# A fused token, state-space and expert kernel: rows of C spread by DMA, scan states in PSUM, and both residual sums moved into TensorE's accumulations

## The chip, the core and the metric

The kernel runs on one core of a Trainium2 chip. The metric is the device time of one execution in microseconds (us), the median of repeated runs; lower is better. Engine names in the profile: PE is TensorE's matmuls and PEld its weight loads, DVE is VectorE, ACT is ScalarE, POOL is GpSimd, SP is the engine that issues the DMAs. `Lnnn` is a line of the kernel.

## What is computed

The whole model is a tokenizer (convolutions over 32 images), a state-space (Mamba) layer with a gated feed-forward part, and a layer of attention with routed experts. The change is in the middle layer. Cut to what matters, for tokens in 32 sequences of 82:

```python
xdbl = z @ W_xproj.T                       # -> dt_in (96), B (16), C (16) per token
dt   = softplus(dt_in @ W_dt.T + b_dt)     # (.., 384)
A_bar = exp(dt[..., None] * A)             # (.., 384, 16)
Bx    = (dt * z)[..., None] * B[:, None, :]
h[t]  = A_bar[t] * h[t-1] + Bx[t]          # the scan, along a sequence
y     = sum_s h[..., s] * C[..., s] + D_skip * z
x1    = xl + y @ W_out.T                   # first residual
x     = (x1 + H) + ffn(rmsnorm(x1))        # second residual, written back to H
```

## The kernel before

Four sequences make a round (328 tokens), so the middle layer has 8 rounds. In a round the 16 states of `y` are taken one after another: 16 *turns*, `s` = 0 to 15. The 384 channels lie as 3 groups of 128 partitions, so one turn handles tiles of 128x984. In turn `s` of round `i`:

- ScalarE writes the decays `exp(dt*A)` of turn `s+2` into two PSUM banks (`decays`, L1198), in two halves. The first half may start once the first half of the scan of turn `s+1` has read the bank, and this scan waits for nothing else there.
- GpSimd multiplies `dtz` with a row of B that a DMA has copied to all partitions (`Bb`), giving `Bx`, three turns ahead (L1450).
- VectorE multiplies the states `hs` with the row of C (*the product*, L1343), then runs the scan of turn `s+1` in two halves of 492 (L1333). `hs` has four buffers in SBUF (`LONG`), so a scan needs no wait for the product just ahead of it. The row of C stands in PSUM, where TensorE has spread it over the partitions with a selecting matmul (`spread_c`, L1030) from a split into three bf16 pieces, `P3`. The pieces are made by ScalarE (L1145, L1149, L1150), VectorE (`R`, L1289) and GpSimd (L1416).
- TensorE adds the product to `y` in PSUM by a matmul with the identity (`add_y`, L1050), and in turn 15 also `D_skip * z` (L1048).

Around this stand the side works of the neighbouring rounds, in an order written out by hand (`program`): in turn `s` of round `i` come `post(s)` of round `i-1` and `pre(s)` of round `i+1`. TensorE and ScalarE do them ahead of their own `step`, VectorE and GpSimd behind it. Every engine works strictly in the order of its list, and semaphores hold it. What the prediction speaks of:

- turn 0: ScalarE copies `y` out of PSUM (`drain`, L1216) when `add_y` of turn 15 is done. TensorE's next `add_y` waits for this copy.
- turn 1: TensorE multiplies `y` with `w_o` into O0 and O1 (L997). VectorE adds `xl` and writes `x1` (L1309). ScalarE makes `hn` for the next round (L1131).
- turn 2: TensorE transposes `hn` (L949), into the banks that O0 and O1 had; it waits until `x1` is taken out. ScalarE scales the result to `hT` (L1103, L1106), and its decays of turn 4 stand behind that.
- turns 3 to 5: `z` (L1285); turn 6: TensorE computes B, C and dt_in (L979) and ScalarE copies them out (L1144 to L1146); turns 8 to 11: softplus, the longer part of it on GpSimd.
- turns 10 to 13: the feed-forward part in four slices, TensorE, then ScalarE's tanh, then VectorE's `th` and `av` (L1314, L1317).
- turn 14: TensorE multiplies `av` with `w_dn` into N0 and N1 (L1022), behind the last `av`. VectorE adds `x1` and writes `H` (L1323) in turns 14 and 15.

The last round has no `pre`, and its `post(14)`, `post(15)` and the whole `post` of the last round follow in a function `ending`, mixed with the first parts of the attention layer. Ahead of the first scan stand VectorE's statistics of 24 images (`chunk_stats`, L1269) and a first `pre` (L1292 to L1302).

## Time and profile before

| | |
|---|---|
| median of 3 runs | 1364.94 us (1364.93 to 1366.9) |
| the profiled execution, own time | 1364.19 us |
| its span, first to last instruction | 1362.2 us |
| the 8 rounds of the middle layer | from 253.01 us (first scan) to 763 us (last product) |
| start of product 0 in rounds 0 to 7 | 255.30, 315.36, 381.38, 446.58, 510.81, 575.87, 640.23, 704.95 us |

The profiled execution is 0.75 us below the median. Rounds 1 to 6 are 64.2 to 66.0 us long each. Within a round no engine is busy all the time; which wait ends last at a place is read from the chain of waits and the timeline.

### The profile page before, as it was taken

How to read it: one execution, taken by the hardware profiler on the slowest of the kernel's cores; microseconds unless marked ns; L12 is line 12 of the kernel's file. 1: busy time of each engine (PE TensorE's matmuls, PEld its weight loads, DVE VectorE, ACT ScalarE, POOL GpSimd, SP SyncE). 2: the span in 40 equal slices, each digit the busy share in tenths (PEclk: the TensorE clock that was granted, in tenths of full speed). 3: DMA queues.
4: the chain of work that ended last, by engine and by line, in shares of the span. 5: the costliest groups of instructions: out<-in, count | busy, mean ns of one | idle time of the engine just before them, and what ended most of it. 6: DMA issues, size and time to landing. Idle time of an engine off the chain costs nothing.

```text
span 1362.2 us, 20654 instructions
## 1 busy us (share of the span) xinstructions
PE 1196.6 (88%) x5844; PEld 759.2 (56%) x5845; DVE 1066.6 (78%) x2275; ACT 710.4 (52%) x1652; POOL 744.2 (55%) x473
## 2 busy tenths in 40 slices
PE   7986867478898989899997789999999889999996
PEld 4432434224454545455452468888888666667674
DVE  5998697998999999999989645677788756666663
ACT  1256431776868777787866334555553462323232
POOL 3047651877878796969697420115545665232322
PEclk9897878698999999999999998999998899999998
DMA  6200002440404041322320025001112133222221
GB/s 186 60 1 0 28 9 63 157 149 1 149 1 149 12 137 39 110 75 74 108 73 1 1 93 186 9 9 25 27 26 56 37 61 54 41 37 39 39 39 21
DMA packets 72573, 81.11 MB, mean 60 GB/s; under 512 B 13450, under 2 KB 65129, under 8 KB 72489
## 3 DMA queue, kind: packets, MB, share of 16 engines
q1 hardware_dynamic: 53154, 69.17, 16.0%
q0 software_dynamic: 17152, 9.24, 5.0%
q10 hardware_dynamic: 2184, 1.72, 0.5%
q8 instruction: 36, 0.59, 0.2%
q14 instruction: 47, 0.39, 0.1%
HBM read 48.75 MB, written 30.01 MB: 58 GB/s over the span
## 4 chain that ended last, share of the span: by engine, by line
PE 56%; DVE 20%; ACT 12%; issue 7%; POOL 2%; DMA 2%; DVEq 1%; SPq 0%; ACTq 0%; POOLq 0%
PE ps L1050 7%; PE ps L2295 6%; DVE hs L1333 5%; PE ps L2273 5%; PE ps L1652 3%; PE ps L1710 3%; PE ps L1022 3%; ACT ps L1198 3%; PE ps L2278 3%; PE ps L277 3%; PE ps L955 2%; PE ps L1725 2%; PE ps L2285 2%; PE ps L270 2%; PE ps L997 2%
## 5 line engine op out<-in xcount | busy, mean ns | idle before, releaser
L1450 POOL TENSOR_TENSOR Bx<-dtz,Bb 128x984 f32<-128x984 f32 x128 | 287.7, 2272 | 47.6 <-DVE hs L1333 34.4
L1333 DVE TENSOR_TENSOR_SCAN hs<-ps,Bx 128x492 f32<-128x492 f32 x256 | 287.7, 1165 | 15.9 <-POOL Bx L1450 12.2
L1050 PE MATMUL ps<-hs,b_id 128*128 128x492 f32 x512 | 236.9, 586 | 8.5 <-ACT y L1216 7.2
L1198 ACT ACTIVATE ps<-dt,A 128x324 f32<-128x324 f32 (+1 forms) x512 | 210.5, 456 | 56.3 <-DVE hs L1333 53.6
L2431 POOL DMA_INDIRECT out<-yt,dest x48 | 74.7, 1556 | 158.9 <-DVE yt L2417 149.2
L2350 ACT ACTIVATE hT__6147<-ps,e_b 128x128 f32<-128x128 f32 x288 | 79.4, 374 | 154.1 <-PE ps L2285 154.0
L1343 DVE TENSOR_TENSOR hs<-hs,ps 128x984 f32<-128x984 f32 x128 | 150.4, 1175 | 2.8 <-issue 0.6
L1050 PEld LDWEIGHTS ps<-hs,b_id 128*128 128x128 f32 x512 | 93.4, 195 | 75.3 <-issue 69.6
L2295 PE MATMUL ps<-W,hT__6147 128*128 x576 | 109.4, 327 | 1.0 <-DVE yb L2411 1.0
L2126 POOL DMA_INDIRECT buckets<-XS,c_slot x64 | 90.6, 1416 | 31.9 <-issue 16.4
L2138 POOL TENSOR_TENSOR c_x<-c_x,bro 82x192 f32<-82x192 f32 x32 | 18.9, 590 | 135.7 <-DVE c_x L1893 135.1
L2295 PEld LDWEIGHTS ps<-W,hT__6147 128*128 128x128 f32 x576 | 91.5, 191 | 1.7 <-issue 1.7
L1030 PE MATMUL ps<-P,sel 128*128 128x328 bf16 x128 | 40.2, 316 | 52.8 <-DVE hs L1343 40.8
L2397 DVE COPY hb<-ps 128x768 f32<-128x768 f32 x41 | 39.3, 958 | 59.2 <-PE ps L2278 58.1
L2273 PE MATMUL ps<-W,xT 128*128 x192 | 78.5, 534 | 6.1 <-DVE xT L2388 2.8
L1866 DVE TENSOR_REDUCE mx<-ps 82x12 f32<-82x984 f32 x32 | 37.7, 1178 | 56.0 <-PE ps L1710 55.3
L1030 PEld LDWEIGHTS ps<-P,sel 128*128 128x128 bf16 x128 | 12.3, 97 | 102.0 <-DVE hs L1343 67.4
L1725 PEld LDWEIGHTS ps<-V,PT 82*82 82x82 f32 x768 | 61.3, 154 | 7.6 <-issue 2.0
L1710 PE MATMUL ps<-kB,qT 128*82 128x328 f32 (+1 forms) x256 | 60.8, 382 | 3.1 <-DVE E L1870 2.0
L1725 PE MATMUL ps<-V,PT 82*82 82x17 f32 x768 | 60.3, 224 | 1.2 <-DVE XN L1900 1.2
...
L207 DVE SCALAR_TENSOR_TENSOR ps<-PF,vec,ps 96x196 f32<-96x196 f32 (+2 forms) x168 | 57.7, 423 | 0.0
...
## 6 DMA issues: line engine op xcount, KB each, us to landing
Bb<-b_rows SPq DMA_DIRECT2D x32, 656.0 KB, 6.8
...
```

Source lines behind the costliest of these rows:

```text
L1050: mm = pe.matmul(ps[:, BANK_Y + h, 0:HALF], ident[:], f2(hs[:, s % LONG])[:, h * HALF:(h + 1) * HALF], start=s == 0, stop=s == STATE - 1)
L1198: a = act.activation(ps[:, BANK_A + h, c:c + w].rearrange("p (g t) -> p g t", t=S)[:, :, 1:S], dt[:, (par + t // STATE) % 2, m, g0 * S:g1 ...
L1333: v.tensor_tensor_scan(f2(hs[:, t % LONG])[:, c], ps[:, BANK_A + h, 0:HALF], f2(Bx[:, t % RING])[:, c], 0.0, ALU.mult, ALU.add).then_inc(s ...
L1343: v.tensor_tensor(hs[:, s % LONG], hs[:, s % LONG], ps[:, BANK_C + s % 2, 0:N].rearrange("p (a n) -> p a n", a=1).broadcast_to([128, NI, N ...
L1450: g.tensor_tensor(Bx[:, t % RING], dtz[:, p], Bb[:, p, t % STATE, :].rearrange("p (a n) -> p a n", a=1).broadcast_to([128, NI, N]), ALU.mu ...
L1710: mm = pe.matmul(ps[0:S, SCORES + h0 // 6, (h0 % 6) * S:(h0 % 6 + h1 - h0) * S], qT[:, par, m_, q * S:(q + 1) * S], kB[:, par, m_, q, j:j ...
L1725: mm = pe.matmul(ps[0:S, HEAD_OUT + c % 2, h * (DH + 1):(h + 1) * (DH + 1)], PT[:, c % 2, h, :], V[:, vpar, c, h, :], start=True, stop=True)
L2126: g.indirect_dma_start(out=xs, out_offset=bass.IndirectOffsetOnAxis(ap=slot[:, p % 2, k, c:c + 1], axis=0), in_=slots(p)[:, c, :], in_offs ...
L2273: pe.matmul(ps[:, UP + h, 0:384], xT[:, p, 0, :], W1[:, bass.ds(e, 1), h * 384:(h + 1) * 384].rearrange("p a n -> p (a n)"), start=True, s ...
L2295: mm = pe.matmul(ps[:, Y, 0:D], hT[:, p, k, :], W2[:, k, bass.ds(e, 1), :].rearrange("p a n -> p (a n)"), start=k == 0, stop=k == KF - 1)
L2350: a = act.activation(hT[:, p, k, :], ps[:, FLIPPED + k // 3, (k % 3) * 128:(k % 3 + 1) * 128], ACT.Gelu, bias=b1[:, k, bass.ds(e, 1)])
L2431: g.indirect_dma_start(out=out, out_offset=bass.IndirectOffsetOnAxis(ap=dest[:, p:p + 1], axis=0), in_=yt[:, p, :], in_offset=None, comput ...
```

## The change

Three things. (1) B and C both go to DRAM (`bc_d`) and come back by DMA to all partitions, in one tile `BC` of four groups, which is now single and not one for each parity of the round; `spread_c`, `P3`, `Pm`, `R`, `sel` and `oh` are gone. (2) The scan writes its states to PSUM banks 2 and 3 (one buffer), and the product writes to `hc` in SBUF (four buffers). The scan of a turn therefore waits for the product ahead of it. (3) The residuals `xl` and `x1` are added by TensorE, as a matmul with the identity at the head of the accumulation (L994 and L1023 of the new file), and ScalarE copies the sums out (L1156 for `x1`, in turn 2; L1181 for `H`, in turn 15); VectorE's four sums of a round are gone. In `ending`, GpSimd's fills of `kB`, `XS` and `inc` wait for the last product.

```diff
         def _(sp):
...
-                sp.wait_ge(s_Bs, j + 1)
+                sp.wait_ge(s_BCs, j + 1)
                 if j >= 2:
                     sp.wait_ge(s_bx, (j - 1) * STATE)
-                sp.dma_start(b_d[par], Bs[:]).then_inc(s_bd, 16)
+                sp.dma_start(bc_d[par], BCs[:]).then_inc(s_bd, 16)
                 sp.wait_ge(s_bd, 16 * (j + 1))
+                rows = bc_d[par].rearrange("(a k g s) n -> a g k s n", a=1, k=2, s=GROUP)
                 for g in range(STATE // GROUP):
-                    rows = slice(g * GROUP, (g + 1) * GROUP)
-                    sp.dma_start(Bb[:, par, rows, :],
-                                 b_d[par, rows, :].rearrange("(a s) n -> a s n", a=1).broadcast_to([128, GROUP, N])).then_inc(s_Bb[g], 16)
+                    if j >= 1:
+                        sp.wait_ge(s_hc, (j - 1) * STATE + (g + 1) * GROUP)
+                    sp.dma_start(BC[:, g], rows[:, g].broadcast_to([128, 2, GROUP, N])).then_inc(s_BC[g], 16)
...
 TensorE, post
                 if s == 1:
-                    pe.wait_ge(s_y, p + 1)
+                    pe.wait_ge(s_xl, (p + 1) * G)
                     for h in range(2):
                         free(f"O{h}", p, other)
+                        pe.matmul(ps[0:S, bank(f"O{h}"), 0:2 * D], ident[0:S, 0:S], xl[:, par, 2 * h:2 * h + 2, :], start=True, stop=False)
+                        if h == 0:
+                            pe.wait_ge(s_y, p + 1)
...
                 if s == 14:
+                    pe.wait_ge(s_add, p + 1)
                     pe.wait_ge(s_av, p * 4 + 4)
                     for h in range(2):
                         if not is_last(p):
                             free(f"N{h}", p, other)
+                        pe.matmul(ps[0:S, wide(f"N{h}", p), 0:2 * D], ident[0:S, 0:S], x1[:, 2 * h:2 * h + 2, :], start=True, stop=False)
...
 TensorE, step
-                if not last or s + 2 < STATE:
-                    spread_c(i, par, s + 2)
                 add_y(i, par, s)
...
 ScalarE, pre(6) and pre(7)
-                    act.activation(Bs[:], ps[96:96 + STATE, bank("X"), 0:N], ACT.Copy).then_inc(s_Bs, 1)
-                    act.activation(P3[96:128, par, :], ps[96:128, bank("X"), 0:N], ACT.Copy).then_inc(s_hi, 1)
+                    act.activation(BCs[:], ps[96:96 + 2 * STATE, bank("X"), 0:N], ACT.Copy).then_inc(s_BCs, 1)
                     act.activation(dtin[:], ps[0:HD, bank("X"), 0:N], ACT.Copy).then_inc(s_dtin, 1)
-                if s == 7:
-                    act.wait_ge(s_R, j + 1)
-                    act.activation(P3[32:64, par, :], R[:], ACT.Copy)
-                    act.activation(Pm[:], R[:], ACT.Copy).then_inc(s_mid, 1)
...
 ScalarE, post
+                if s == 2:
+                    for h in range(2):
+                        act.wait_ge(s_o, p * 2 + (h + 1))
+                        act.activation(x1[:, 2 * h:2 * h + 2, :].rearrange("p j c -> p (j c)"), ps[0:S, bank(f"O{h}"), 0:2 * D], ACT.Copy).then_inc(s_x1, 1)
...
+                if s == 15:
+                    for h in range(2):
+                        act.wait_ge(s_dn, p * 2 + (h + 1))
+                        act.activation(H[:, bass.ds(p * G + 2 * h, 2), :].rearrange("p j c -> p (j c)"), ps[0:S, wide(f"N{h}", p), 0:2 * D], ACT.Copy).then_inc(s_H, 1)
...
 ScalarE, ending
             def ending(last):
+                post(last - 1, 0, 15, None)
                 drain(last)
+                post(last, 1, 2, None)
                 post(last, 1, 3, None)
...
 VectorE, post(1), post(14), post(15), pre(6) and the cast of sel in tail: removed; scan and step
                     if h == 0:
                         v.wait_ge(s_bx, i * STATE + (t + 1))
-                        at_least(v, s_ys, i * STATE + (t - LONG + 1))
+                        at_least(v, s_hc, i * STATE + t)
                     c = slice(h * HALF, (h + 1) * HALF)
-                    v.tensor_tensor_scan(f2(hs[:, t % LONG])[:, c], ps[:, BANK_A + h, 0:HALF], f2(Bx[:, t % RING])[:, c],
+                    v.tensor_tensor_scan(hs[:, c], ps[:, BANK_A + h, 0:HALF], f2(Bx[:, t % RING])[:, c],
                                          0.0, ALU.mult, ALU.add).then_inc(s_scan, 1)
...
                 v.wait_ge(s_scan, 2 * (i * STATE + s) + 2)
-                v.wait_ge(s_pc, i * STATE + (s + 1))
-                v.tensor_tensor(hs[:, s % LONG], hs[:, s % LONG],
-                                ps[:, BANK_C + s % 2, 0:N].rearrange("p (a n) -> p a n", a=1).broadcast_to([128, NI, N]),
+                at_least(v, s_ys, i * STATE + (s - LONG + 1))
+                v.tensor_tensor(hc[:, s % LONG], hs.rearrange("p (a n) -> p a n", a=NI),
+                                BC[:, s // GROUP, 1, s % GROUP, :].rearrange("p (a n) -> p a n", a=1).broadcast_to([128, NI, N]),
                                 ALU.mult).then_inc(s_hc, 1)
...
 GpSimd, ending
-                fr.fills(g)
+                fr.fills(g, lambda: g.wait_ge(s_hc, ROUNDS * STATE))
```

How the lists of the engines change is shown at three places. First TensorE at turns 14 and 15. Before, from the `w_dn` matmuls to the last `add_y` of the round:

```order
L1022 MATMUL ps<-wdn,av 82x192 x16
L640 REGISTER_ALU
L1030 MATMUL ps<-P_120,sel 128x328
L1050 MATMUL ps<-hs,b_id 128x492 x2
L640 REGISTER_ALU
L1030 MATMUL ps<-P_120,sel 128x328
L1048 MATMUL ps<-z,skip 128x328
L1048 MATMUL ps<-z,skip 128x164 x2
L1048 MATMUL ps<-z,skip 128x328
L1050 MATMUL ps<-hs,b_id 128x492 x2
```

After (`x_130` is `x1`, `b_id` the identity):

```order
L1023 MATMUL ps<-x_130,b_id 82x384
L1027 MATMUL ps<-wdn,av 82x192 x8
L1023 MATMUL ps<-x_130,b_id 82x384
L1027 MATMUL ps<-wdn,av 82x192 x8
L1037 REGISTER_ALU
L1046 MATMUL ps<-hc,b_id 128x492 x2
L1037 REGISTER_ALU
L1044 MATMUL ps<-z,skip 128x328
L1044 MATMUL ps<-z,skip 128x164 x2
L1044 MATMUL ps<-z,skip 128x328
L1046 MATMUL ps<-hc,b_id 128x492 x2
```

Two identity matmuls of 384 columns have come in, and two selecting matmuls of 328 bf16 columns are gone. The second place is TensorE at turns 0 and 1 of the next round. Before:

```order
L640 ISA
L1030 MATMUL ps<-P_120,sel 128x328
L1050 MATMUL ps<-hs,b_id 128x492 x2
L942 REGISTER_ALU
L997 MATMUL ps<-wo,y 82x192 x6
L942 REGISTER_ALU
L997 MATMUL ps<-wo,y 82x192 x6
L640 REGISTER_ALU
L1030 MATMUL ps<-P_120,sel 128x328
L1050 MATMUL ps<-hs,b_id 128x492 x2
```

After:

```order
L1037 ISA
L1046 MATMUL ps<-hc,b_id 128x492 x2
L991 REGISTER_ALU
L942 REGISTER_ALU
L994 MATMUL ps<-xl,b_id 82x384
L1000 MATMUL ps<-wo,y 82x192 x6
L942 REGISTER_ALU
L994 MATMUL ps<-xl,b_id 82x384
L1000 MATMUL ps<-wo,y 82x192 x6
L1037 REGISTER_ALU
L1046 MATMUL ps<-hc,b_id 128x492 x2
```

Again two identity matmuls more, here in the middle of the `w_o` matmuls, and two selecting ones fewer. The third place is ScalarE behind the last decays of the last round. Before:

```order
L1216 ACTIVATE y<-ps 128x984
L1172 ACTIVATE hf,b_ss<-x_135 82x192 x4
L1175 ACTIVATE b_ms<-b_ss 82x4
L1179 ACTIVATE hf<-x_135,b_rr 82x192 x4
L732 ACTIVATE qb<-vec 128x3
```

After:

```order
L1181 ACTIVATE H<-ps 82x384 x2
L1209 ACTIVATE y<-ps 128x984
L1156 ACTIVATE x_130<-ps 82x384 x2
L1161 ACTIVATE hf,b_ss<-x_130 82x192 x4
L1164 ACTIVATE b_ms<-b_ss 82x4
```

The copies of `H`, which wait for the `w_dn` matmuls, now stand ahead of the copy of `y`, for which the `w_o` matmuls wait.

## Rows read from the trace of the kernel before

**Rows 1.** Windows: stretch, its us, busy us (instructions) PE, PEld, DVE, ACT, POOL; PE clock, DMA share, GB/s.

```profile
303.00:319.00 16.00, 11.78 (x24) 5.30 (x22) 12.40 (x12) 6.91 (x16) 15.92 (x8) 0.57 0.00 1
...
446.60:510.80 64.20, 59.00 (x228) 31.99 (x227) 60.09 (x64) 47.81 (x114) 51.59 (x25) 1.00 0.25 79
```

**Rows 2.** Chain of waits, round 1 into round 2: start us, us, what.

```profile
372.42 0.51 DVE av L1317
...
373.06 5.40 PE ps L1022 x32
378.46 0.14 PE ps L1030
...
383.73 1.00 ACT y L1216
...
384.87 1.89 PE ps L1050 x4
386.76 3.90 PE ps L997 x24
...
390.80 1.65 PE ps L1050 x4
```

**Rows 3.** Timeline behind it: start us, us, engine line op tiles [idle before].

```profile
390.69 0.55 DVE L1309 TENSOR_TENSOR x<-xl,ps 82x384 f32<-82x384 f32 x1 [1.40 <-PE ps L997]
...
394.43 1.63 ACT L1198 ACTIVATE ps<-dt,A 128x324 f32<-128x324 f32 x4
...
395.63 2.25 DVE L1333 TENSOR_TENSOR_SCAN hs<-ps,Bx 128x492 f32<-128x492 f32 x2
```

**Rows 4.** Timeline of VectorE, turns 9 and 10 of round 1.

```profile
349.49 2.25 DVE L1333 TENSOR_TENSOR_SCAN hs<-ps,Bx 128x492 f32<-128x492 f32 x2 [0.29 <-ACT ps L1198]
351.78 1.18 DVE L1343 TENSOR_TENSOR hs<-hs,ps 128x984 f32<-128x984 f32 x1
352.88 2.25 DVE L1333 TENSOR_TENSOR_SCAN hs<-ps,Bx 128x492 f32<-128x492 f32 x2
```

**Rows 5.** Groups by form: count, busy us, mean ns, idle ahead and releasers.

```profile
L1333 DVE TENSOR_TENSOR_SCAN hs<-ps,Bx 128x492 f32<-128x492 f32 x256 | 287.7, 1165 | 15.9 <-POOL Bx L1450 12.2 <-ACT ps L1198 3.6
...
L207 DVE SCALAR_TENSOR_TENSOR ps<-P,vec,ps 128x196 f32<-128x196 f32 x168 | 56.4, 421 | 0.0
...
L207 DVE SCALAR_TENSOR_TENSOR D<-P,vec,ps 128x196 f32<-128x196 f32 x24 | 8.9, 413 | 0.0
L1309 DVE TENSOR_TENSOR x<-xl,ps 82x384 f32<-82x384 f32 x16 | 8.7, 549 | 13.8 <-PE ps L997 13.8
```

**Rows 6.** Timeline of VectorE ahead of the first scan.

```profile
229.14 1.40 DVE L508 SCALAR_TENSOR_TENSOR P<-P,rs,rows 105x192 f32<-105x192 f32 x4
233.70 0.50 DVE L1289 TENSOR_TENSOR R<-ps,P 32x328 f32<-32x328 f32 x1 [3.16 <-ACT P L1145]
...
234.34 2.17 DVE L1269 BATCH_NORM_STATS2 b_st<-H 82x6 f32<-82x192 f32 x8
...
244.42 0.73 DVE L1292 TENSOR_SCALAR ax<-u 128x984 f32<-128x984 f32 x1
```

**Rows 7.** Timeline of the ending.

```profile
749.01 6.66 POOL L683 MEMSET kB<- 128x7872 f32 x1
...
766.49 5.37 PE L1022 MATMUL ps<-wdn,av 128*82 128x192 f32 x32
766.69 0.99 ACT L1216 ACTIVATE y<-ps 128x984 f32<-128x984 f32 x1 [8.14 <-PE ps L1050]
...
771.68 4.07 PE L997 MATMUL ps<-wo,y 128*82 128x192 f32 x24
...
775.62 2.91 POOL L704 TENSOR_TENSOR c_root<-c_root,c_nh 82x16 f32<-82x16 f32 x1 [18.45 <-DVE c_root L698]
...
779.59 1.49 ACT L1179 ACTIVATE hf<-x,b_rr 82x192 f32<-82x192 f32 x4 [1.90 <-POOL b_rr L1435]
```

**Rows 8.** DMAs of 233 to 262 us: KB each, median us from issue to landing.

```profile
Bb<-b_rows SPq DMA_DIRECT2D x4, 656.0 KB, 6.6
```

More of the change, by code:

```diff
@@ L773, in attention_front, with mamba @@
     return fr
-def mamba(nc, ctx, block, at, ps, tok, fr, H, vec, ident, w_zg, w_x, w_dt, a_log, w_o, w_ug, w_dn, onehot, b_d, xs):
+def mamba(nc, ctx, block, at, ps, tok, fr, H, vec, ident, w_zg, w_x, w_dt, a_log, w_o, w_ug, w_dn, bc_d, xs):
     if True:
@@ L997, in post @@
                                 mm = pe.matmul(ps[0:S, bank(f"O{h}"), q * D:(q + 1) * D], y[:, k * N + c:k * N + c + S], wo[:, k, :],
-                                               start=k == 0, stop=k == NI - 1)
+                                               start=False, stop=q == 1 and k == NI - 1)
                         mm.then_inc(s_o, 1)
@@ L1022, in post @@
                                 mm = pe.matmul(ps[0:S, wide(f"N{h}", p), q * D:(q + 1) * D], av[:, k, c:c + S], wdn[:, k, :],
[L1023 removed]
+                                               start=False, stop=q == 1 and k == NF - 1)
                         mm.then_inc(s_dn, 1)
[L1026 to L1031 removed]
             def first():
@@ L1070, in ending @@
                 post(last - 1, 0, 14, None)
-                post(last - 1, 0, 15, None)
                 post(last, 1, 1, None)
@@ L1088, in ending @@
                 post(last, 1, 14, None)
-                post(last, 1, 15, None)
                 pe.wait_ge(fr.s_qT, 3)
@@ L1114, in softplus_in @@
             def softplus_in(j, m):
-                if isinstance(j, int) and j == 0 and m == 0:
-                    act.wait_ge(s_cst, 2)
                 act.wait_ge(s_dtp, j * 3 + (m + 1))
@@ L1252, in ending @@
                 fr.keep_keys(act, 0, 0, 2, fr.place)
+                post(last, 1, 15, None)
             tok.scalar(act, tail)
@@ L1364, in tail @@
                     v.wait_ge(tok.s_lr, CH)
-                    v.memset(P3[64:96], 0.0)
                     v.memset(ps[:, BANK_A:BANK_A + 2, :], 0.0).then_inc(s_cst, 1)
@@ L1391, in ending @@
                 post(last, 1, 13, None)
-                post(last, 1, 14, None)
-                post(last, 1, 15, None)
                 v.wait_ge(s_H, 2 * ROUNDS + 2)
```

95 lines of the change are left out of this document (30 added, 65 removed).

## The prediction

> **What bounds the kernel now.** I read the windows first. In a middle round both TensorE (59.0 of 64.2 us) and VectorE (60.1) are nearly full [rows 1], so busy shares don't decide. The chain of waits does, and it changes engines inside a round. From VectorE's last `av` of turn 13 the chain leaves VectorE: TensorE's `w_dn` matmuls (5.40 us), `add_y` of turns 14 and 15, ScalarE's copy of `y` (1.00), `add_y` of turn 0 (1.89) and the `w_o` matmuls (3.90), up to 390.66 us [rows 2]. Only then can VectorE form `x1`: it has stood idle 1.40 us ahead of the second sum [rows 3], and 13.8 us ahead of all 16 of them [rows 5]. In the timeline the decays of turn 4 come at 394.43, and the scan of turn 4 at 395.63 uses them with hardly 0.4 us to spare [rows 3]. From there to turn 13 VectorE sets the pace: product, scan, scan, with 3.39 us from scan to scan where nothing is added [rows 4]. So a round is a cycle of two parts: TensorE's part, from `av` of turn 13 to the scan of turn 4, and VectorE's part, from that scan to turn 13.
>
> **The price of one identity matmul.** The trace has the same operation at 492 columns: `add_y`, two of them (four records) in 1.65 us [rows 2], so 1.68 ns a column, and 384 columns take 0.645 us. A round gets four of them, 2.6 us. A selecting matmul in bf16, which goes, is 0.14 us [rows 2]. Both at full clock.
>
> **TensorE's part, rounds 1 to 6.** (a) At turn 14 two identities stand behind the wait for the last `av`, so nothing hides them: +1.29, less two selecting matmuls ahead of the copy of `y`: -0.28. The copy of `y` comes 1.0 us later. (b) In turn 1 two more identities: the first could run before `y` is there, but `add_y` of turn 0 is ahead of it and waits for the same copy. +1.29. (c) Behind the `w_o` matmuls the old path was the sum of `x1`, product 2, scan 3, product 3, scan 4: 390.66 to 395.63, 4.97 us. This path is cut, since `x1` is now ScalarE's. The one beside it stays: `add_y` of turn 1, transposes of `hn`, `hT`, decays of turn 4. From that `add_y`'s start (390.80) to the decays (394.43) is 3.63; half of their 1.63 serves the first half scan: 0.82, and 0.05 for a semaphore: 4.50 us [rows 2, 3]. The copies of `x1` (0.5 us each is taken, between the 0.41 a decay of 243 columns averages, 1.63 over four [rows 3], and the 1.00 of the copy of 984 [rows 2]) end before the transposes want their banks. So -0.47. In all +1.29 - 0.28 + 1.29 - 0.47 = +1.83 us a round. VectorE's savings in turns 14 to 2 (sums of `H`, sums of `x1`, the wait) go into this wait: from the end of `av` at 372.93 its own new pace would reach scan 4 after five turns of 3.5, 1.2 of a product and at most 1.5 that GpSimd holds scan 15 (12.2 us in 8 times [rows 5]), 20.2 us in all; TensorE's path to 395.63 was 22.7, and becomes 24.5.
>
> Five such crossings: +9.2. The one from round 0 has no `w_dn` matmuls: 1.29 - 0.47 = +0.8. The one into the last round has no `hn` behind it; there ScalarE can do the decays right behind its copies (0.5 + 0.82 + 0.15 against 4.97): 1.01 + 1.29 - 3.5 = -1.2.
>
> **VectorE's part.** The scan now waits for the product ahead. Before, it began 1.10 us behind the product's start, although the product lasts 1.18; between scan and product, where a wait stands, the gap is 0.04 past the end [rows 4]. So 1.18 + 0.04 - 1.10 = +0.12 a turn. Writing PSUM instead of SBUF costs 8 ns (421 against 413 for one form [rows 5]), twice a turn. Together +0.14. The product had an operand in PSUM before and has one now; no change taken. In turns 4 to 13 this is 10 x 0.14 = +1.4; in turn 12 one 0.14 is hidden, since `th` waits for ScalarE's table loads anyway; `R` goes (-0.5 [rows 6]), and with the two `P3` copies out of ScalarE's turn 7 the wait of 0.29 ahead of scan 9 goes, with 0.1 of restart. Sum +0.36 for each of six rounds: +2.2. Round 0: 9 turns x 0.14 - 0.5 up to softplus, then GpSimd's chain fixes the time, then two turns: +0.9. Last round, turns 4 to 15: +1.5.
>
> On this wait the Trainium skill speaks against me (VectorE: DVE Perf Modes, "The DRAIN you can't avoid"): the next operation doesn't begin until the pipe is empty, and a semaphore behind each operation cost nothing extra there. By this rule the turn would grow by 0.02 instead of 0.14. The rows show otherwise: without a wait 0.08 before the recorded end, with it 0.04 after [rows 4]. The sum goes by the rows; what the rule would make of the time is rival 3.
>
> **Ahead of the first scan.** VectorE idles 3.16 us for `R` at 233.70, and only then begins the statistics at 234.34 that it must finish before softplus at 244.42 [rows 6]. Without `R` and a memset of 0.5 they begin at 230.1: -4.2, and a little more since GpSimd's last piece of `P3` no longer runs beside the last product: -4.4. The next to be late would be ScalarE's `u`, which I place 0.4 us before it is wanted. GpSimd wants the first rows of B when softplus and `dtz` are through, one short and four operations of 1.2 us behind 240: near 246. The four DMAs are issued near 235 and are twice as large, so 6.6 us grows to some 13 for the median one [rows 8], less for the first. Bounds: -2 if all four land together, -5.
>
> **The ending.** TensorE: two identities, +1.29. ScalarE's copies of `H` stand ahead of the copy of `y`, and the second waits for the last `w_dn` matmul: before, `y` was copied at 766.69, under those matmuls; now it is done at 766.49 + 5.2 + 1.3 + 0.5 + 1.0 + 0.1, 774.6, and the `w_o` matmuls start 3.0 later than 771.68 [rows 7]. With one more identity the end of them is 3.65 later. `x1` copied in series, less 0.75 us that GpSimd's roots held up the norm before: `hf`, 779.59 before, comes 3.3 later. Everything up to the last `w_dn` matmuls hangs on it; these get 1.29. Sum +4.6; bounds 2.6 (identities alone) and 6. The fills moved behind the last product (`kB` 6.66 and, an estimate, 1.6 of smaller ones) end near 771.5; GpSimd had 18.45 us idle up to 775.62 [rows 7], so they are hidden, by 4 us.
>
> **Sum.** -4.4 + 0.9 + 0.8 + 9.2 + 2.2 - 1.2 + 1.5 + 4.6 = +13.6. On the profiled execution's own 1364.19 that is 1377.8; it lies 0.75 below the median, so 1378. Own range of this case 1370 to 1385 (start -5 to -2, ending 2.6 to 6, crossings 1.2 to 2.4, turn 0.10 to 0.20).
>
> **Rivals.** 0.2%, 2.7 us, is about what can be told from no change.
> 1. *Faster, VectorE's time counts* (0.08). If TensorE's path were not what the scan of turn 4 waits for, a middle round would lose the sums and their wait, 2.6 us, and gain only the 0.14s: about -2.3 x 6 - 4.4 + 3, 1349. It decides from the point at which TensorE's path falls under 20.2 us; it stands at 24.5, so 4.3 us are missing. For it: VectorE is the fuller engine [rows 1]. Against: the idle of 13.8 us, which TensorE ends [rows 5].
> 2. *The clock* (0.12). Between 303 and 319 us, with TensorE busy for 11.78 of 16 us, its granted clock is 0.57, so the lower of the two levels, 1.2 GHz, was granted for most of it [rows 1]. Rounds 0 and 7 and the ending have longer gaps now: selecting matmuls gone, turns longer. If the last round's end runs at 1.2 GHz, skip and `add_y` (1.65 each) and `w_dn` (5.2) take up to twice their 8.5 us; taking most of that, +7: 1385. The Trainium skill (TensorE: Matmul & The Clock Gate, "What's actually happening") has idle engines fall to 1.2 GHz too.
> 3. *The wait costs nothing* (0.06): 0.02 in place of 0.14 a turn: 58 + 10 + 12 turns x 0.12 less, 9.4: 1368.
> 4. *Rows late* (0.06): the DMAs of doubled size hold GpSimd at the start: 1382. Later rounds have 25 us for the first group.
> 5. *Gains and losses cancel* (0.06): crossings at +0.3 because ScalarE's transposed rows come earlier than I have them: 1366.
>
> My forecast has the remaining 0.62. Faster: rival 1 and a third of 5 and some unknown, 0.11; same 0.06; slower 0.83. The range, 1362 to 1386, leaves out rival 1 and the far end of 2.
>
> **What the profile after would show.** Right: VectorE's idle ahead of L1309 replaced by an idle of 3 to 4 us ahead of the scan of turn 4, ended by ScalarE; turn to turn 3.5 us; middle rounds of 66.8; first scan near 248.6; identities of 0.65 us; the `y` copy of the last round ending near 784 (774.6 and the 9 us up to there). Wrong, if that idle isn't there and the scans of turns 2 to 4 follow at 3.5 us, if the scan's duration grows by more than 20 ns, or if TensorE's clock in round 7 is below 1.

## The result and the profile after

The changed kernel takes 1395.1 us (median of four runs, 1392.1 to 1396.2); the kernel before, run beside it, 1365.9. The ratio is 1.020, 95% interval 1.017 to 1.024: slower. Forecast were 1378 and a range of 1362 to 1386, so the direction was right and the size short by 17 us, outside the range. The profiled execution of the new kernel took 1396.2 us with a span of 1393.6, against 1364.2 and 1362.2 before.

I cut both traces at VectorE's products, whose starts are easy to find, and compared piece by piece. The new kernel's timeline of VectorE at the start of round 0, which answers to [rows 4]:

```profile
246.03 1.18 DVE L1323 TENSOR_TENSOR hc<-ps,BC 128x984 f32<-128x984 f32 x1
247.35 2.26 DVE L1313 TENSOR_TENSOR_SCAN ps<-ps,Bx 128x492 f32<-128x492 f32 x2
249.65 1.18 DVE L1323 TENSOR_TENSOR hc<-ps,BC 128x984 f32<-128x984 f32 x1
```

From product to product it is 3.62 us where it was 3.38, and from a product's start to the scan behind it 1.32 where it was 1.10. The groups of the page, answering to [rows 5], show that the operations themselves hardly changed, and that idle time moved to the scan:

```profile
L1313 DVE TENSOR_TENSOR_SCAN ps<-ps,Bx 128x492 f32<-128x492 f32 x256 | 289.6, 1177 | 67.9 <-ACT ps L1191 50.2
...
L1323 DVE TENSOR_TENSOR hc<-ps,BC 128x984 f32<-128x984 f32 x128 | 150.8, 1178 | 4.3
```

The chain of waits at the crossing from round 1 to round 2, answering to [rows 2]:

```profile
365.99 0.51 DVE av L1304
366.50 0.14 issue
366.64 0.84 PE ps L1023 x2
367.48 2.60 PE ps L1027 x16
370.08 0.65 PE ps L1023 x2
...
378.33 1.00 ACT y L1209
...
381.35 0.65 PE ps L994 x2
382.00 1.95 PE ps L1000 x12
383.95 0.65 PE ps L994 x2
384.60 1.95 PE ps L1000 x12
386.55 1.65 PE ps L1046 x4
```

From the end of `av` to the copy of `y` it is 11.83 us against 10.80 before, from there to the end of the `w_o` matmuls 8.22 against 6.93: two identities each time, in the first stretch less two selecting matmuls. The timeline behind it, answering to [rows 3]; the sums of `x1` are now ScalarE's copies, and the scan of turn 4 waits for ScalarE:

```profile
384.08 0.47 ACT L1156 ACTIVATE x<-ps 82x384 f32<-82x384 f32 x1
...
386.59 0.49 ACT L1156 ACTIVATE x<-ps 82x384 f32<-82x384 f32 x1 [2.04 <-PE ps L1000]
...
390.18 1.62 ACT L1191 ACTIVATE ps<-dt,A 128x324 f32<-128x324 f32 x4
391.22 2.26 DVE L1313 TENSOR_TENSOR_SCAN ps<-ps,Bx 128x492 f32<-128x492 f32 x2 [3.82 <-ACT ps L1191]
```

This crossing I had foreseen. What I had not is seen one round later, in ScalarE's timeline at the start of round 3:

```profile
441.47 1.61 ACT L1191 ACTIVATE ps<-dt,A 128x324 f32<-128x324 f32 x4
452.35 0.99 ACT L1209 ACTIVATE y<-ps 128x984 f32<-128x984 f32 x1 [9.26 <-issue]
453.23 1.61 ACT L1191 ACTIVATE ps<-dt,A 128x324 f32<-128x324 f32 x4
```

For 9.26 us ScalarE waits for nothing that the profile shows ("issue"). Everything hangs on this copy of `y`, and VectorE stands still for 8.14 us. Two rounds later, at 595.48, the same row has 9.32. At 378.33 and 521.40, the starts of rounds 2 and 4, it has 2.87, ended by TensorE. The loop's body holds two rounds, so the engines branch back to its head exactly at the starts of rounds 3 and 5. The view of DMA queues for 444 to 453 us says what else goes on there:

```profile
DMA  9998899999999999999999999999999999610001
...
q1 hardware_dynamic: 2918, 2.71, 94.5%
q14 instruction: 3, 0.02, 0.8%
```

Three packets of instructions share the 16 DMA engines with 2.71 MB of data: the rows of group 3 and the zero fill, both issued at the round's end, near 439 us, because SyncE now waits for the last products of the round. In the kernel before, the rows of a round (656 KB a group) and the fill were all issued in its middle (409.8 to 411.8 us in round 2).

The start, answering to [rows 6]. `R` is gone, and the statistics follow the first stage at once:

```profile
223.74 0.48 DVE L1281 SCALAR_TENSOR_TENSOR z<-sg,ps 128x328 f32<-128x328 f32 x1
...
225.54 2.16 DVE L1265 BATCH_NORM_STATS2 b_st<-H 82x6 f32<-82x192 f32 x8
...
235.63 0.73 DVE L1285 TENSOR_SCALAR ax<-u 128x984 f32<-128x984 f32 x1
...
243.74 2.26 DVE L1313 TENSOR_TENSOR_SCAN ps<-ps,Bx 128x492 f32<-128x492 f32 x2 [2.51 <-POOL Bx L1419]
```

The ending, answering to [rows 7]:

```profile
788.21 6.66 POOL L684 MEMSET kB<- 128x7872 f32 x1 [14.94 <-DVE hc L1323]
...
798.32 0.49 ACT L1181 ACTIVATE H<-ps 82x384 f32<-82x384 f32 x1 [2.76 <-PE ps L1027]
798.71 0.98 ACT L1209 ACTIVATE y<-ps 128x984 f32<-128x984 f32 x1
...
807.77 1.49 ACT L1168 ACTIVATE hf<-x,b_rr 82x192 f32<-82x192 f32 x4 [1.11 <-POOL b_rr L1404]
```

The last product starts at 786.97 (761.84 before), so `hf` is 3.05 us later than it was. The whole, in us, all from starts of products and the spans:

| piece | before | after | change | forecast |
|---|---|---|---|---|
| up to the last `z` of the first stage (nothing changed but one memset, 0.5, that is gone) | 228.73 | 223.74 | -5.0 | -0.5 |
| from there to the first product | 26.57 | 22.29 | -4.3 | -3.9 |
| round 0, to product 0 of round 1 | 60.06 | 61.85 | +1.8 | +0.9 |
| round 1, product 0 to 4 | 18.10 | 18.28 | +0.2 | +0.8 |
| product 4 to 14, rounds 1 to 6 | 39.37 | 40.24 | 6 x 0.87 | 6 x 0.36 |
| product 14 to product 4 of the next, five times | 25.35 | 27.38 | 5 x 2.03 | 5 x 1.83 |
| the same, at the loop's two edges, on top | 0 | 7.8, 8.0 | +15.8 | 0 |
| product 14 of round 6 to 4 of round 7 | 25.08 | 23.73 | -1.4 | -1.2 |
| round 7, product 4 to 15 | 40.34 | 42.89 | +2.5 | +1.5 |
| last product to the end of the span | 600.4 | 606.6 | +6.3 | +4.6 |

The sum is +31.4, the difference of the spans. The prediction's -4.4 for the start stands in the first two rows, since it counted the memset. Its +0.8 for the crossing out of round 0 stands in the fourth row; taken whole, from product 14 to product 4, this crossing went from 28.41 to 28.34 us.

### The profile page after: what moved, and what is told of

It reads as the page before. It is cut to its first block, busy times and chain, and to the rows that moved or that the text cites. A ratio compares the mean times of both kernels' runs of the same rounds, so it can differ in the third digit from the quotient of the medians.

```text
span 1393.6 us, 20450 instructions
## 1 busy us (share of the span) xinstructions
PE 1208.5 (87%) x5780; PEld 761.7 (55%) x5781; DVE 1060.2 (76%) x2233; ACT 716.8 (51%) x1660; POOL 737.6 (53%) x465
## 4 chain that ended last, share of the span: by engine, by line
PE 54%; DVE 24%; issue 10%; ACT 7%; DMA 2%; POOL 2%; DVEq 1%; SPq 0%; ACTq 0%; POOLq 0%
DVE ps L1313 6%; PE ps L2264 6%; DVE hc L1323 5%; PE ps L1046 5%; PE ps L2242 5%; PE ps L1621 3%; PE ps L1679 3%; PE ps L1027 3%; PE ps L2247 3%; PE ps L1694 3%; PE ps L2254 2%; PE ps L277 2%; PE ps L955 2%; PE ps L1000 2%; PE ps L270 2%
## 5 line engine op out<-in xcount | busy, mean ns | idle before, releaser
L1313 DVE TENSOR_TENSOR_SCAN ps<-ps,Bx 128x492 f32<-128x492 f32 x256 | 289.6, 1177 | 67.9 <-ACT ps L1191 50.2
L1419 POOL TENSOR_TENSOR Bx<-dtz,BC 128x984 f32<-128x984 f32 x128 | 288.0, 2274 | 86.9 <-DVE ps L1313 55.2
L1046 PE MATMUL ps<-hc,b_id 128*128 128x492 f32 x512 | 248.4, 610 | 69.9 <-DVE hc L1323 48.9
L1191 ACT ACTIVATE ps<-dt,A 128x324 f32<-128x324 f32 (+1 forms) x512 | 213.8, 457 | 41.1 <-DVE ps L1313 37.0
L1046 PEld LDWEIGHTS ps<-hc,b_id 128*128 128x128 f32 x512 | 91.4, 195 | 181.6 <-issue 116.0
L1323 DVE TENSOR_TENSOR hc<-ps,BC 128x984 f32<-128x984 f32 x128 | 150.8, 1178 | 4.3
L955 PE MATMUL ps<-hfT,wug 128*128 128x328 f32 x128 | 45.3, 478 | 20.4 <-DVE av L1304 18.9
L207 DVE SCALAR_TENSOR_TENSOR ps<-P,vec,ps 128x196 f32<-128x196 f32 x168 | 56.4, 420 | 0.0
```

The source lines that it names most:

```text
L207: i = eng.scalar_tensor_tensor(flat(dst[:, k, cols]) if t == 8 else acc, tap(src, k, c, t, a, b), w, acc, ALU.mult, ALU.add)
L1046: mm = pe.matmul(ps[:, BANK_Y + h, 0:HALF], ident[:], f2(hc[:, s % LONG])[:, h * HALF:(h + 1) * HALF], start=s == 0, stop=s == STATE - 1)
L1191: a = act.activation(ps[:, BANK_A + h, c:c + w].rearrange("p (g t) -> p g t", t=S)[:, :, 1:S], dt[:, (par + t // STATE) % 2, m, g0 * S:g1 ...
L1313: v.tensor_tensor_scan(hs[:, c], ps[:, BANK_A + h, 0:HALF], f2(Bx[:, t % RING])[:, c], 0.0, ALU.mult, ALU.add).then_inc(s_scan, 1)
L1323: v.tensor_tensor(hc[:, s % LONG], hs.rearrange("p (a n) -> p a n", a=NI), BC[:, s // GROUP, 1, s % GROUP, :].rearrange("p (a n) -> p a n" ...
L1419: g.tensor_tensor(Bx[:, t % RING], dtz[:, p], BC[:, t % STATE // GROUP, 0, t % GROUP, :].rearrange("p (a n) -> p a n", a=1).broadcast_to([ ...
```

## The experiments

Two effects had to be told apart, the stalls at the loop's edges and the sizes of the three parts of the change, which I call: part 1, rows of B and C by DMA; part 2, states in PSUM, and with them the scan's wait for the product ahead; part 3, residuals on TensorE with ScalarE's copies. Ratios are to the kernel before, with their 95% intervals.

### The stalls at the loop's edges

**a1_late_rows.** The changed kernel, group 3 and the fill behind it four turns later:

```diff
-                        sp.wait_ge(s_hc, (j - 1) * STATE + (g + 1) * GROUP)
+                        sp.wait_ge(s_hc, (j - 1) * STATE + (g + 1) * GROUP + (4 if g == 3 else 0))
```

> The changed kernel with one number changed: from round 1 on SyncE waits four products longer before it issues the rows of group 3, and so the zero fill behind them, so that neither transfer runs while the engines branch back to the loop's head (starts of rounds 3 and 5). Theory A, these two transfers hold back the engines behind the branch: the stalls of 7.8 and 8.0 us are gone, both crossings take 67.6 us like the others, and the time is 1395.1 - 15.8 = 1379 (1377 to 1382). Theory B, the stalls belong to the loop's new body and not to the transfers: 1395 (1393 to 1397). Theory C, rows issued in turn 4 come too late for the inputs of turn 12: the scans of turn 12 wait and it is over 1385.

Measured 1383.1 us, ratio 1.016 (1.008 to 1.023); the runs of this group scatter, and the interval overlaps the changed kernel's, so I read the traces. The crossing at the first edge fell from 35.2 us to 27.7 and that at the second from 35.4 to 27.4, where it is 27.4 without an edge. All other pieces are the same to 0.1 us, but for the start (+0.2) and the ending (-0.3). ScalarE's timeline at the same place, and the DMA queues from 442 to 450 us:

```profile
441.73 1.62 ACT L1191 ACTIVATE ps<-dt,A 128x324 f32<-128x324 f32 x4
446.53 0.99 ACT L1209 ACTIVATE y<-ps 128x984 f32<-128x984 f32 x1 [3.18 <-PE ps L1046]
```

```profile
DMA  0000000000000010000000000100000000000000
...
q14 instruction: 3, 0.02, 1.0%
```

Again three packets of instructions, now alone. Theory A holds, B falls, and the rows were not late (C).

**a2_fill_early.** The changed kernel, with the fill issued ahead of group 2 instead, in turn 8:

```diff
+                    if j >= 1 and g == 2:
+                        sp.dma_start(xs[j * part:(j + 1) * part, :]..., zero[:]...).then_inc(s_zf, 16)
                     if j >= 1:
                         sp.wait_ge(s_hc, (j - 1) * STATE + (g + 1) * GROUP)
```

> The changed kernel with the zero fill of 2288 KB issued ahead of the rows of group 2 (turn 8 of the round before), the rows of group 3 (1312 KB) still at the round's end. Theory A in the form that the amount queued at the branch sets the stall: 1312 of 3600 KB remain, landing some 7 us after issue and so about when the branch comes, so 0 to 3 us remain of each 7.9: 1379 to 1386. Theory A in the form that any transfer at the branch costs the whole: 1395. Theory B (the loop's body): 1395.

Measured 1384.4, ratio 1.015 (1.008 to 1.021). The two crossings have 3.8 and 1.5 us on top, against 7.8 and 8.0. ScalarE's row at the first edge:

```profile
447.21 0.99 ACT L1214 ACTIVATE y<-ps 128x984 f32<-128x984 f32 x1 [4.92 <-issue]
```

With less under way the stall is smaller. How it grows with the amount is not shown: at the first edge the last of the 1312 KB's packets starts at 443.77, only 1.5 us after ScalarE's decays have ended (442.29), and in other bodies 3.8 to 4.3 us are found with no data at all (a3, c1 to c3 below).

**b2_fill_at_edge, b4_fill_at_branch, b5_fill_over_fetch.** The same question put to the kernel before, which has only the fill to move. SyncE issues it behind product 16, 14 or 15 of the round before:

```diff
+                if j >= 1:
+                    sp.wait_ge(s_hc, j * STATE)        # b4: - 2, b5: - 1
                 part = BUCKET_ROWS // ROUNDS
```

> The kernel before with one wait more: the zero fill of 2288 KB of each round from round 1 on is issued only when the last product of the round before is done, where the changed kernel issues it. Theory A: the old loop then stalls too at the starts of rounds 3 and 5, by 4 to 8 us each, 1366 + 8 to 16 = 1374 to 1382. Theory B: 1366, within 1.

> The kernel before with the zero fill of 2288 KB issued when product 14 of the round before is done, about 8 us before the branch (in the run with the fill after product 16 the fill's packets began at 443.9, when one instruction packet had just gone). Theory A, instruction packets queue behind whatever fills the 16 DMA engines: ScalarE's first instruction behind the branch comes late, 3 to 6 us at each of two edges, 1366 + 6 to 12 = 1372 to 1378. Theory A', only the rows (read from DRAM into SBUF) delay them: 1366, within 1.

> The kernel before with the zero fill issued when product 15 of the round before is done, so that its 13 us of packets begin some 5 us before ScalarE's branch (its fetch is then behind 2288 KB, where before it came first or after). Theory A: y copy late at two edges, 4 to 6 us each, 1366 + 8 to 12 = 1375. Theory A', only rows read from DRAM and written to SBUF delay it: 1366 within 1.5.

Ratios 1.001 (0.997 to 1.004), 0.998 (0.996 to 1.000) and 1.003 (1.000 to 1.005): theory A's number failed three times. In b2 the fill's packets ran from 444.6 to 453.1 us, when one instruction packet had just gone; the next started at 450.79, 3.8 us later than in the kernel before (446.95), and ScalarE's copy of `y` had not waited for it (448.52, before 448.45). In b4 they ran from 433.0 to 441.3, ahead of the branch. b5 shows why they cost next to nothing; its own two edge crossings are 0.6 us longer each. VectorE's row at the first edge:

```profile
444.82 0.53 DVE L1325 TENSOR_TENSOR H<-x,ps 82x384 f32 x1
448.01 1.18 DVE L1345 TENSOR_TENSOR hs<-hs,ps 128x984 f32<-128x984 f32 x1 [2.67 <-issue]
```

In the kernel before the same idle is 0.40:

```profile
446.58 1.18 DVE L1343 TENSOR_TENSOR hs<-hs,ps 128x984 f32<-128x984 f32 x1 [0.40 <-issue]
```

So the fill does hold back an engine that branches under it, here VectorE by 2.3 us; but in this kernel VectorE waits for TensorE a turn later anyway (turn 1 to 2 shrinks from 5.9 to 4.3 us), and ScalarE, which TensorE waits for, branches when the fill's packets come to their end (its last decays end at 445.79, the last packet starts at 446.38) and has 1.83 ahead of its copy as before.

**f1_in_place_edge** is d1, a kernel described further below (states in place in PSUM, no wait), with rows and fill back at the round's end:

```diff
-                        sp.wait_ge(s_hc, (j - 1) * STATE + (g + 1) * GROUP + (4 if g == 3 else 0))
+                        sp.wait_ge(s_hc, (j - 1) * STATE + (g + 1) * GROUP)
```

> The kernel with in-place states and no wait, with the rows of group 3 and the zero fill back at the round's end as in the changed kernel. Theory A, the stall belongs to the transfers over the fetch and not to one layout of the loop: ScalarE's copy of y at the starts of rounds 3 and 5 has 8 to 10 us ahead of it instead of 3, 1349 + 12 to 16 = 1363 (1359 to 1366). Rival, it needs the changed kernel's layout: 1349 to 1352.

Measured 1357.3, ratio 0.995 (0.993 to 0.997), against 0.989 for d1. ScalarE's row at the first edge has 6.92 where d1 has 3.18, ended by TensorE:

```profile
445.32 0.99 ACT L1196 ACTIVATE y<-ps 128x984 f32<-128x984 f32 x1 [6.92 <-issue]
```

The edge crossings take 31.0 and 31.6 us where d1's take 25.7 and 25.5, so 5.3 and 6.1 more. The stall came back in another loop body, so it belongs to the transfers; but it is smaller than expected (8 to 10 us ahead of the copy), and the time lies below theory A's range.

The traces also have a time for every packet, and these tie the stall to the instructions. In the changed kernel the second instruction packet at the edge follows the first by 5.1 us both times (445.56 and 450.66, 588.72 and 593.79), in a1 by 2.1. In f1 the two are 6.0 and 5.9 us apart, in d1 2.1. At all 14 edges of this study at which ScalarE's idle ahead of the copy of `y` is ended by "issue", the copy starts 1.0 to 1.3 us behind the end of an instruction packet (451.02 and 452.35 in the changed kernel).

### The three parts

**b1_wait_only.** The kernel before with one wait more:

```diff
                         at_least(v, s_ys, i * STATE + (t - LONG + 1))
+                        at_least(v, s_hc, i * STATE + t)
```

> The kernel before with one wait more: each scan waits for the semaphore of VectorE's own product of the turn before; states stay in SBUF, nothing else changes. In the changed kernel a static turn takes 3.61 us against 3.38 and VectorE's part of a middle round 0.88 us more. Theory D, that is the wait alone: the gap from the product to the scan grows from 1.10 to about 1.3 and the time is 1366 + 6 x 0.9 + 1.8 + 1.6 = 1375 (1372 to 1377). Theory E, it is the writing of the states to PSUM, or the reading of them: 1366 to 1368. The rule that such a wait costs nothing also gives 1366.

Measured 1380.5, ratio 1.011 (1.005 to 1.018): 15 us (16.8 between the profiled spans), more than any theory had. Its turn:

```profile
355.80 1.18 DVE L1344 TENSOR_TENSOR hs<-hs,ps 128x984 f32<-128x984 f32 x1
357.11 2.25 DVE L1334 TENSOR_TENSOR_SCAN hs<-ps,Bx 128x492 f32<-128x492 f32 x2
359.40 1.18 DVE L1344 TENSOR_TENSOR hs<-hs,ps 128x984 f32<-128x984 f32 x1
```

1.31 from product to scan, 3.60 a turn. The wait alone is 0.22 a turn, and the PSUM writing next to nothing. From product 4 to 14 it costs 1.6 a round, not the 0.87 of the changed kernel, in which part 1 gives half of it back.

**c1_rows_only, c3_rows_wait, a3_rows_psum, c2_rows_resid.** Rows of B and C by DMA, late as in a1, in all four. c1 keeps the states in the old ring in SBUF with no wait; c3 adds the wait; a3 has PSUM states and the wait; these three have the residual sums on VectorE. c2 is c1 with part 3. The core of c1 against a1:

```diff
-                        at_least(v, s_hc, i * STATE + t)
+                        at_least(v, s_ys, i * STATE + (t - LONG + 1))
-                    v.tensor_tensor_scan(hs[:, c], ps[:, BANK_A + h, 0:HALF], ...
+                    v.tensor_tensor_scan(f2(hc[:, t % LONG])[:, c], ps[:, BANK_A + h, 0:HALF], ...
...
-                v.tensor_tensor(hc[:, s % LONG], hs.rearrange("p (a n) -> p a n", a=NI),
+                v.tensor_tensor(hc[:, s % LONG], hc[:, s % LONG],
```

> Part 1 alone: rows of B and C by DMA (group 3 late, as in the run before), but the states in the old ring of four in SBUF, multiplied in place, no wait for the product, and both residual sums on VectorE as before. Theory F, the loss lies in parts 2 and 3 and the rows of C are a gain: first scan 4 to 9 us earlier, no waits for a selecting product, turn 3.38, VectorE's part of a middle round 38.5 instead of 39.37, crossings 0.3 to 0.5 shorter: 1366 - 5 - 5.5 - 3 = 1352 (1349 to 1358), faster than both kernels. Theory G, the rows themselves cost (twice the DMA traffic, VectorE reading rows from SBUF): 1366 or more.

> Parts 1 and 3 without part 2: as c1, with the identity products of both residuals and ScalarE's copies. Theory H, part 3 costs what the accounting gives (two identities and the ScalarE handover, 1.7 us for each of six crossings on TensorE's side of it less VectorE's sums, and 5 us in the ending): c1 + 10 to 14 us. Rival: part 3 is nearly free while no wait makes the turn longer, since the crossing is bound elsewhere: c1 + 5 (the ending alone).

> Parts 1 and 2 without part 3: rows late, states in two banks of PSUM with the wait for the product, residual sums on VectorE. Theory D/H: c1 + 0.22 for each of some 90 turns that VectorE bounds = c1 + 14 to 18 (1367 to 1372), and the kernel with all three parts and late rows (1383 here) is above this by part 3. If parts 2 and 3 share a cost (the ring's slack that the wait uses up), a3 + c2 - c1 comes out over that kernel's time.

> As c1, and each scan waits for the product before it; states stay in SBUF. Theory D, the wait alone is the cost of part 2: the same as a3 within 2 us, turn 3.60. Theory E, the PSUM states cost of their own: a3 is over 3 us above this one.

Measured: c1 1447.2, ratio 1.061 (1.056 to 1.066); c2 1453.2, 1.063 (1.059 to 1.068); c3 1457.6, 1.067 (1.063 to 1.071); a3 1374.3, 1.005 (1.003 to 1.008). c3 and a3 differ by 83 us in the direction that no theory had, although a turn of c3 in which the product takes its 1.18 us is the 3.60 that theory D gave. Theory F fell by 95 us: c1, which I expected to be the fastest, is among the slowest. Its timeline in round 1, VectorE and then GpSimd, and the page's groups:

```profile
342.22 1.18 DVE L1318 TENSOR_TENSOR hc<-hc,BC 128x984 f32<-128x984 f32 x1
...
345.86 4.52 DVE L1318 TENSOR_TENSOR hc<-hc,BC 128x984 f32<-128x984 f32 x1
```

```profile
344.85 4.49 POOL L1419 TENSOR_TENSOR Bx<-dtz,BC 128x984 f32<-128x984 f32 x2
```

```profile
L1419 POOL TENSOR_TENSOR Bx<-dtz,BC 128x984 f32<-128x984 f32 x128 | 349.2, 2743 | 89.3 <-DVE hc L1309 63.1
...
L1318 DVE TENSOR_TENSOR hc<-hc,BC 128x984 f32<-128x984 f32 x128 | 256.8, 2006 | 2.1
```

The product, with both operands and its result in SBUF, takes 1.18 us beside an idle GpSimd and 4.52 beside two of its multiplications (the longest of the run is 5.03); it ends about one product's length after they do (349.34). GpSimd's own grow from 2274 to 2743 ns. With one operand in PSUM, as in both kernels of this study, it is 1.18 in every turn. The trace of before had a small sign of this: ahead of the first scan VectorE's `dtz`, with all three tensors in SBUF, took 1.67 us while GpSimd made its last piece of `P3`, and 1.18 in the changed kernel, where that piece is gone. The Trainium skill has this contention between GpSimd and a VectorE instruction with two SBUF inputs (GPSIMD Engine Reference, "Specifications"); by that rule the trace agrees, and the price is the measured one. So parts 1 and 2 aren't separable: once the rows of C are in SBUF, the states must be in PSUM. Together, with late rows, they cost a3's 0.5%, 7 us; in its trace 3.4 and 3.0 of them are the two edges, which this loop body has even without traffic (ScalarE's row at the first has 4.03 ended by issue).

c2 is the miss of theory H: it is 6 us above c1, where the theory had 10 to 14 and its rival 5. A middle crossing takes 27.6 us against c1's 28.0; part 3 costs 5.2 us in the ending, and the two edges have 5.6 and 4.2 us on top for 3.1 each. In a kernel whose VectorE is slowed like this the identities of the middle crossings are hidden. That the slow products are the reason is argued, not shown.

**b3_resid_only.** The kernel before with part 3 alone (the edits of part 3 in the diff of the change, word for word):

```diff
+                        pe.matmul(ps[0:S, bank(f"O{h}"), 0:2 * D], ident[0:S, 0:S], xl[:, par, 2 * h:2 * h + 2, :], start=True, stop=False)
...
+                        pe.matmul(ps[0:S, wide(f"N{h}", p), 0:2 * D], ident[0:S, 0:S], x1[:, 2 * h:2 * h + 2, :], start=True, stop=False)
...
+                        act.activation(x1[...], ps[0:S, bank(f"O{h}"), 0:2 * D], ACT.Copy).then_inc(s_x1, 1)
...
+                        act.activation(H[...], ps[0:S, wide(f"N{h}", p), 0:2 * D], ACT.Copy).then_inc(s_H, 1)
```

> The kernel before with part 3 alone: both residuals as identity products on TensorE, sums copied out by ScalarE, nothing else changed. Theory H, the accounting by parts holds: between the two kernels with late rows and PSUM states a crossing without a loop edge takes 25.48 us with the sums on VectorE and 27.38 with part 3, so +1.9 for each of five middle crossings, about +1 around the first and the last, and +4.6 to 6 in the ending: 1366 + 9.5 + 1 + 5 = 1381 (1378 to 1384). Rival, part 3 costs only where the wait of part 2 has used up VectorE's slack: the ending alone, 1371.

Measured 1382.8, ratio 1.014 (1.011 to 1.018), near theory H's time; the rival's 1371 falls. Theory H's price of a crossing fails, though: crossings take 28.1 us against 25.35, 2.8 more where it had 1.9 (2.4 at the edges). Product 4 to 14 is unchanged at 39.4 to 39.5, and last product to end is 607.2 against 600.4.

**d1_in_place.** If the wait is the cost of part 2, the states can stay in PSUM without it: decays alternate between two pairs of banks (the second was free once the selecting matmuls were gone), and the scan writes its states over its own decays.

```diff
-                        at_least(v, s_hc, i * STATE + t)
-                    v.tensor_tensor_scan(hs[:, c], ps[:, BANK_A + h, 0:HALF], f2(Bx[:, t % RING])[:, c],
+                    v.tensor_tensor_scan(hs[t % 2][:, c], hs[t % 2][:, c], f2(Bx[:, t % RING])[:, c],
...
-                    at_least(act, s_scan, 2 * (i * STATE + t) + (h - 1))
+                    if h == 0:
+                        at_least(act, s_hc, i * STATE + (t - 1))
...
+                    first = f2(dt[:, par]).rearrange("p (g t) -> p g t", t=S)[:, :, 0]
+                    g.tensor_tensor(first, first, big[:], ALU.add).then_inc(s_col, 1)
```

> Parts 1 and 2 without the wait: decays go alternately to two pairs of PSUM banks, the scan writes its states over its decays in the same pair, and the product reads them there; so a scan no longer waits for the product before it, and the decays of turn t+2 wait for product t. The zero decay at each sequence's start, overwritten now, is made by adding 1000 to the step size of the first position after its use (one small GpSimd operation a round); rows of group 3 late, residual sums on VectorE. Theory D, the wait was the cost of part 2: turn back to 3.38 to 3.40, 0.22 less for each of some 78 turns that VectorE bounds, a3 - 17 = 1374 - 17 = 1357 (1354 to 1362), faster than both kernels by 0.6%. Rival, reading and writing of states in PSUM, or the stalls of 3 us at two loop edges, hold: 1366 to 1374.

Measured 1349.3 (1344.4 to 1351.1, six runs), ratio 0.989 (0.986 to 0.992): 1.1% faster than the kernel before and 3% than the changed one. VectorE's turn, and its groups:

```profile
348.15 1.18 DVE L1322 TENSOR_TENSOR hc<-ps,BC 128x984 f32<-128x984 f32 x1
349.25 2.25 DVE L1312 TENSOR_TENSOR_SCAN ps<-ps,Bx 128x492 f32<-128x492 f32 x2
```

```profile
L1312 DVE TENSOR_TENSOR_SCAN ps<-ps,Bx 128x492 f32<-128x492 f32 x256 | 288.5, 1172 | 15.5 <-POOL Bx L1426 15.3
...
L1322 DVE TENSOR_TENSOR hc<-ps,BC 128x984 f32<-128x984 f32 x128 | 150.6, 1177 | 2.7
```

1.10 from product to scan again, although both now work in PSUM, and 3.39 a turn, as theory D says. The time is 8 us under its number and below its range. Against a3, the six middle parts give 14.3 us and the two edges 5.3 that the theory didn't count, and the ending is 4.6 shorter, of which I have no account (f1, with the same ending, has only 1.3 of it).

**d2_in_place_resid.** d1 with part 3.

> All three parts with late rows, but the states in place and no wait. Theory H, part 3 costs the same in any of these kernels: d1 + 1.9 for each of five crossings + 4 to 5 in the ending = 1349 + 14 = 1363 (1360 to 1366). Rival, with more slack on VectorE and ScalarE part 3 is partly hidden: 1349 + 5 to 9.

Measured 1360.8, ratio 0.999 (0.996 to 1.001). Crossings 27.3 us against d1's 25.1, last product to end 605.3 against 597.7, product 4 to 14 the same 37.9. Part 3 takes back most of what d1 gained, and its price is little changed without the wait (theory H).

The pieces side by side, in us (crossing: product 14 to product 4 of the next round, where there is no edge; edges: on top of it):

| kernel | parts | 4 to 14 | crossing | edges | round 7, 0 to 15 | last product to end |
|---|---|---|---|---|---|---|
| before | | 39.37 | 25.35 | 0, 0 | 56.9 | 600.4 |
| after | 1 2 3 | 40.24 | 27.38 | 7.8, 8.0 | 59.5 | 606.6 |
| a1 | 1 2 3 | 40.27 | 27.38 | 0.3, 0 | 59.5 | 606.4 |
| a2 | 1 2 3 | 40.27 | 27.38 | 3.8, 1.5 | 59.5 | 604.6 |
| a3 | 1 2 | 40.26 | 25.48 | 3.4, 3.0 | 60.4 | 602.3 |
| b1 | the wait | 40.96 | 25.79 | 0, 0 | 60.5 | 599.3 |
| b3 | 3 | 39.4 | 28.14 | -0.35, -0.35 | 56.5 | 607.2 |
| c1 | 1 | 47.0 | 28.0 | 3.1, 3.1 | 63.0 | 602.1 |
| c2 | 1 3 | 47.1 | 27.6 | 5.6, 4.2 | 61.1 | 607.3 |
| c3 | 1, the wait | 48.3 | 27.2 | 3.9, 4.9 | 64.5 | 602.4 |
| d1 | 1, in place | 37.88 | 25.10 | 0.7, 0.4 | 56.3 | 597.7 |
| d2 | 1, in place, 3 | 37.87 | 27.33 | 0.1, 0 | 55.7 | 605.3 |
| f1 | 1, in place | 37.87 | 25.09 | 5.9, 6.5 | 56.3 | 601.0 |

## Why the prediction was right in direction and short in size

**What bounds the kernel: right.** The idle of the scan of turn 4, 3.82 us, ended by ScalarE, is where the prediction put it, with what it named as its cause. Rival 1 (VectorE's time counts) is out: part 3 takes work off VectorE, and yet b3 and d2 lengthen every crossing but the one into the last round, as forecast. (It doesn't in c2, where VectorE is slowed otherwise.)

**Identities and copies in the crossing: right, and right for its own reason.** Forecast +1.83, measured +2.03: 1.03 for the copy of `y`, 1.29 to the end of `w_o`, and -0.30 behind it, where I had -0.47. Since b1 shows that the wait adds 0.4 to a crossing too, the match could have been an accident; a1 less a3 says no, 1.90 of it is part 3. In other surroundings it is 2.2 (d2 less d1) or 2.8 (b3). The crossing out of round 0 has -0.1 for the forecast +0.8: part 3 costs 0.6 there (a1 less a3), and the other two parts give 0.7 back (a3 less before), which the prediction did not have.

**The turn: the step failed in size.** "Together +0.14", of which 0.12 the wait. It is 0.22 (b1), with or without PSUM. I took the gap between a scan and its product (0.04) for that between a product and the scan. It is 0.14 there. The chain shows steps of VectorE's queue at this place; that they are the reason, since the scan has several semaphores to pass, I only argue. Over six middle parts this was +5.2 where I had +2.2, in round 0 +1.8 for +0.9, in round 7 +2.5 for +1.5. Rival 3 (the wait costs nothing) is refuted by b1 with 15 us.

**What the rows of C give back: not in the sum.** I had counted `R` and one wait. a3 less b1 is -0.7 from product 4 to 14, and c3 less a3 shows what the change avoided by moving the states: 83 us. The prediction said of the product "no change taken", which held only because an operand of it stays in PSUM.

**The DMAs: this is the step that failed.** The prediction asked of the moved transfers only whether the rows come in time (rival 4; they do, in every run) and not what else uses the DMA engines at the new hour. SyncE's wait for the products moved the fill (2288 KB) and the last group of rows (now 1312 KB, half of it the new rows of C) from the middle of a round to its end, where at every second round ScalarE comes back from the loop's branch. That cost 7.8 and 8.0 us, a term the prediction put at nothing; without it the profiled execution would have been at 1380, inside the range. a1 takes them away, a2 leaves 3.8 and 1.5, f1 brings 5.3 and 6.1 back into a kernel that didn't have them. That it is the fetch of instructions that waits is read from "issue" and the times of the packets of the instruction queue (5.1 us apart for 2.1, and the copy 1.0 to 1.3 us behind one); b5's VectorE shows it for the fill alone, off the path. Which packet was whose, no view tells. The Trainium skill says that a taken branch to a far target needs a fetch of instructions by DMA before the engine goes on (Runtime: NRT & Kernel Launch, "Instruction fetch mechanics"). The traces agree, down to the 4.0 us of a3 without traffic; I had not weighed it. That data traffic lengthens it is what these runs add.

**The start: right.** -4.8 for -4.4, with 0.5 of a memset that is gone and 4.3 behind it. That the first product came 9.3 earlier has another source too: the stage ahead of it, with the same instructions otherwise, ends at 222.7 to 230.3 us in the profiled executions of this study (223.7 after, 228.7 before, 224.3 in b3, 226.2 in b4, 230.3 in f1). What decides this is open. Here it was worth -4.5 and hid as much of the terms that I had too small.

**The ending: +6.3 for +4.6.** `hf` came 3.05 later (3.3 forecast). The first scores of the next stage come 4.9 us later counted from the last product, so the remaining 1.4 lies where nothing changed; d1 and f1, alike there, differ by 3.3.

**The clock (rival 2): not in play.** In the windows, TensorE's granted clock is full throughout round 7, and in the stretch of time that had 0.57 before [rows 1] it is 0.89. The work of that stretch stands 7.5 us earlier now, and there (295.5 to 311.5) it is 0.79. From the last product to the copy of `y` it is 1.00.

```profile
303.00:319.00 16.00, 12.43 (x45) 8.23 (x46) 15.10 (x15) 9.66 (x23) 14.54 (x8) 0.89 0.78 231
727.00:787.00 60.00, 46.76 (x146) 22.11 (x144) 55.34 (x55) 33.35 (x84) 34.39 (x19) 1.00 0.26 77
```

In sum the profiled kernel lies 17.8 us over the +13.6 of the forecast: 15.8 from the edges, 6.5 from the other terms, on balance sized too small (the turn most of all), and -4.5 from the first stage, which was luck.
